# Two superblocks of a pair take turns over the shared blocks of x in the sort stage of a graph network kernel

## The reference

```python
# layer 0: a gated cell on summed messages, then a layer norm
src_h = h[src] @ W_msg.T + b_msg
msg = src_h + edge_embed[clip(edge_type)]
messages = segment_sum(msg, dst, N)
x = layernorm(x + gru_cell(messages, h))
# three further layers
ee = ea @ enc_w + enc_b
agg = segment_sum(concat(x[src], ee), dst, N)
h = relu(bn(agg @ w1 + b1)) @ w2 + b2
# with self loops; the result is layernorm(x + h)
```

## Time and profile before

| | us |
|---|---|
| median of 3 runs | 7135.25 |
| lowest, highest | 7131.29, 7141.64 |
| the profiled execution, its time | 7139.24 |
| its span | 7137.2 |
| first transpose of a unit starts | 273.7 |
| last scatter of the sort starts | 2344.6 |
| loads of the gathered records start | 2347.5 |

### The profile page before, as it was taken

How to read it: one execution, slowest core, us unless ns; L and a number is a source line. 1 busy time by engine, 2 the same in 40 slices (tenths; PEclk the granted TensorE clock), 3 DMA queues, 4 the chain that set the end, 5 groups by cost and what they waited for, 6 DMA issues and landing times.

```text
span 7137.2 us, 82504 instructions
## 1 busy us (share of the span) xinstructions
PE 5870.9 (82%) x29016; PEld 2854.1 (40%) x29152; DVE 3267.2 (46%) x8030; ACT 1370.1 (19%) x2496; POOL 5097.1 (71%) x4958
## 2 busy tenths in 40 slices
PE   2577777666677377767599999999999999999999
PEld 1233333333333143333344444444455444445444
DVE  5666666655565486676544444432222222222222
ACT  1233333333334121121111111110000000000000
POOL 3766666666667477777577777777777777777775
PEclk9998898888989587777699999999999999999999
DMA  6699999999999433333477778778878888778776
GB/s 222 161 238 245 236 240 239 244 240 243 250 242 254 121 99 97 99 99 98 137 240 240 236 229 247 236 242 258 243 233 254 245 243 269 240 241 241 242 240 191
DMA packets 1463508, 1536.87 MB, mean 215 GB/s; under 512 B 820755, under 2 KB 1202772, under 8 KB 1463100
## 3 DMA queue, kind: packets, MB, share of 16 engines
q1 hardware_dynamic: 1250604, 1182.45, 58.4%
q0 software_dynamic: 212496, 349.08, 19.2%
HBM read 1082.27 MB, written 281.76 MB: 191 GB/s over the span
## 4 chain that ended last, share of the span: by engine, by line
PE 53%; POOL 5%; DVE 3%; DMA 2%; issue 2%; ACT 1%; SPq 0%; ACTq 0%; DVEq 0%
PE ps L2502 34%; PE ps L2473 6%; POOL BIG L2556 5%; PE ps L2447 2%; PE ps L2446 2%; PE ps L2359 1%; PE ps L2431 1%; PE ps L2360 1%; PE ps L2453 1%; DMA XT<-rec_q 1%; PE ps L2454 1%; PE ps L2398 1%; DVE BIG L1883 1%; PE ps L2361 1%; DMA RECL<-rec_q 1%
## 5 line engine op out<-in xcount | busy, mean ns | idle before, releaser
L2574 POOL DMA_INDIRECT GL<-h_gathered,IDXA x2646 | 2700.7, 1021 | 919.5 <-issue 770.4
L2502 PE MATMUL ps<-MS,HP 128*128 128x512 bf16 (+1 forms) x11700 | 2712.0, 376 | 27.8 <-DMA MS<-counts 16.1
L2541 POOL DMA_INDIRECT rec_q<-BIG x1563 | 1562.7, 1000 | 777.5 <-issue 470.2
L2502 PEld LDWEIGHTS ps<-MS,HP 128*128 128x128 bf16 x11700 | 1132.7, 98 | 1251.9 <-issue 117.1
L2300 PE MATMUL ps<-MT,XPS 128*128 128x512 bf16 x3763 | 1082.7, 397 | 490.8 <-ACT MT L2102 281.0
L2556 POOL DMA_INDIRECT BIG<-x_parts,SRCq x739 | 828.9, 1122 | 290.1 <-issue 222.8
L2102 ACT CAST MT<-ps 128x512 bf16<-128x512 f32 x1274 | 735.9, 586 | 971.3 <-PE ps L2286 823.9
L1960 DVE TENSOR_REDUCE ROW<-ps 128x128 f32<-128x384 f32 x294 | 163.0, 554 | 1517.6 <-PE ps L2473 1517.6
L2300 PEld LDWEIGHTS ps<-MT,XPS 128*128 128x128 bf16 x3822 | 373.7, 101 | 983.9 <-ACT MT L2102 433.5
L2473 PE MATMUL ps<-GL,SL 128*128 128x384 bf16 (+1 forms) x2646 | 593.9, 333 | 26.0 <-DVE SL L1926 26.0
L2286 PE MATMUL ps<-BIG 128*128 128x512 bf16 x1197 | 470.1, 393 | 44.6 <-DVE BIG L1748 30.1
(11 more groups left out here) (198 smaller groups left out, 4982.6 us busy)
## 6 DMA issues: line engine op xcount, KB each, us to landing
MS<-counts SPq DMA_DIRECT2D x936, 512.0 KB, 4.7
counts<-BIG SPq DMA_DIRECT2D x312, 512.0 KB
XPS<-x_parts SPq DMA_DIRECT2D x312, 384.0 KB, 5.0
GL<-h_gathered,IDXA POOLq DMA_INDIRECT x2646
rec_q<-BIG POOLq DMA_INDIRECT x1563
rec_q<-BIG SPq DMA_DIRECT2D x44, 490.0 KB, 15.2
HTI<-h_cols SPq DMA_DIRECT2D x72, 256.0 KB, 5.9
BIG<-rec_q SPq DMA_DIRECT2D x13, 980.0 KB, 6.5
```

What stands on the lines that cost most here:

```text
L2502: got = t.matmul(bank[:, 0:w].rearrange("p (b c) -> p b c", c=P), HP[:, d, part, :], MS[:, i % MR, 0:x.nb, d % MB, :], start=d + part == 0 ...
L2541: g.indirect_dma_start(out=RAd, out_offset=bass.IndirectOffsetOnAxis(ap=POSI[:, c:c + 1], axis=0), in_=RECA[q % 3][:, c - a, :], in_offset ...
L2574: g.indirect_dma_start(out=GL[:, r % LR, i, 0:3 * P], out_offset=None, in_=HGd[lay], in_offset=bass.IndirectOffsetOnAxis(ap=IDXA[:, a + i: ...
```

## The change

Units are no longer numbered superblock by superblock. Superblocks 0 and 1, 2 and 3, up to 10 and 11 form pairs, and the units of a pair alternate: unit 0 of the first, unit 0 of the second, unit 1 of the first, and so on. Both use the same blocks of x, so one load serves both (`load`), and is issued at the first of the two. Superblock 12 has no partner. The sums of even superblocks stand in bank 6 and those of odd ones in bank 7, and ScalarE copies both at the next pair's first unit. The records of a pair come by halves, of 52 and of 46 cells of both superblocks (`HU` = 13 units), in buffers that are a little larger. Since a pair needs the records of its second superblock too, units begin in window 4 instead of window 3, and `PACE` is 47, so that windows hold 15 or 16 units and none is left after the last window.

```diff
-PACE = 44
+PACE = 47
+HU = 13
+class Unit:
+    def __init__(self, j, u, c0):
+        self.j, self.u, self.c0 = j, u, c0
+        self.n = min(4, NB - 4 * u)
+        self.pair = j // 2
+        self.load = SG * self.pair + u
+        self.half = 2 * self.pair + (u >= HU)
+        self.at = 4 * (u % HU)
+        self.first = j % 2 == 0
+def units():
+    got, c = [], 0
+    for j in range(0, JX, 2):
+        for u in range(SG):
+            for k in range(j, min(j + 2, JX)):
+                got.append(Unit(k, u, c))
+                c += got[-1].n
...
 def beside():
-            if w.q >= LAG:
+            if w.q > LAG:
                 work += PACE / w.groups
-            while m < SG * J and work >= (3 if m < SG * JX else 1) and m // SG <= w.q - LAG:
+            while m < len(UNITS) and work >= 3 and 2 * UNITS[m].pair + 1 <= w.q - LAG:
...
 def cells_scalar(s, m):
-                if u == 0 and i == 1 and 1 <= j <= JX:
-                    sums_scalar(s, j - 1)
+                if x.u == 0 and x.first and x.pair and i == 1:
+                    for j in range(x.j - 2, x.j):
+                        sums_scalar(s, j)
...
 def sums_tensor(t, c):
-                got = t.matmul(PS[7][:, :], XPS[:, m % 3, e % 4, part, :], ...
+                got = t.matmul(PS[6 + x.j % 2][:, :], XPS[:, x.load % 3, i, part, :], ...
...
 def cell_records_sync(y, k):
+            first = k // 2 * 2
+            if k % 2 == 0:
+                for q in range(max(0, first - 1), first + 3):
+                    y.wait_ge(scat[q % 3].sem, scattered(q))
...
 def cells_sync(y, m):
-            if u == 18 and j + 1 < J:
-                cell_records_sync(y, j + 1)
-            if m + 2 < SG * JX:
-                blocks_sync(y, m + 2)
+            if x.first:
+                if x.u == 4:
+                    cell_records_sync(y, 2 * x.pair + 1)
+                if x.u == 18 and 2 * x.pair + 2 < JX:
+                    cell_records_sync(y, 2 * x.pair + 2)
+                if x.load + 2 <= UNITS[-1].load:
+                    blocks_sync(y, x.load + 2)
```

More of the change, by code:

```diff
@@ L133, with last_unit, cells_to @@
 CARRY = carries()
+class Unit:
[7 more added lines that the diff above has]
+        self.first = j % 2 == 0
+        self.turn = None
+def units():
[5 more added lines that the diff above has]
+                c += got[-1].n
+    for s, x in enumerate(x for x in got if x.j < J):
+        x.turn = s
+    return got
+UNITS = units()
+TURNED = [x for x in UNITS if x.turn is not None]
+CELLS = [(m, i) for m, x in enumerate(UNITS) for i in range(x.n)]
+def last_unit(test):
+    return max(m for m, x in enumerate(UNITS) if test(x))
+def cells_to(m):
+    return UNITS[m].c0 + UNITS[m].n
 def beside():
@@ L141, in beside @@
             here = []
-            if w.q >= LAG:
+            if w.q > LAG:
                 work += PACE / w.groups
-            while m < SG * J and work >= (3 if m < SG * JX else 1) and m // SG <= w.q - LAG:
-                work -= 3 if m < SG * JX else 1
+            while m < len(UNITS) and work >= 3 and 2 * UNITS[m].pair + 1 <= w.q - LAG:
+                work -= 3
                 here.append(m)
@@ L148, in beside, with loaded, unit_turned @@
             at.append(here)
-    return at, list(range(m, SG * J))
+    return at, list(range(m, len(UNITS)))
 UNIT_AT, UNIT_REST = beside()
 XAT = {6 + 2 * i: i for i in range(SG)}
[L156 to L164, removed]
+def loaded(k):
+    return 16 * sum(min(2, JX - 2 * (e // 2)) for e in range(k % 2, k + 1, 2))
+def unit_turned(s):
+    return 16 * (s // 2 + 1)
 def scattered(q):
@@ L1471, in program @@
         RECA = [big(64 * RW).rearrange("p (c w) -> p c w", w=RW) for _ in range(3)]
-        recs0 = big(2 * NB * RW)
-        RECS = [recs0[:, NB * RW * i:NB * RW * (i + 1)].rearrange("p (c w) -> p c w", w=RW) for i in range(2)]
-        DSF = [big(NB) for _ in range(2)]
+        recs0 = big(2 * 2 * 4 * HU * RW)
+        RECS = [recs0[:, 8 * HU * RW * i:8 * HU * RW * (i + 1)].rearrange("p (j c w) -> p j c w", j=2, w=RW) for i in range(2)]
+        DSF = [big(8 * HU).rearrange("p (j c) -> p j c", j=2) for _ in range(2)]
         OHS = [big(GT * 64).bitcast(BF16).rearrange("p (c b) -> p c b", b=P) for _ in range(3)]
@@ L1730, in cells_vector @@
         def cells_vector(v, m):
[L1731 to L1736, removed]
+            x = UNITS[m]
+            k, par = x.half, x.j % 2
+            if x.at == 0 and x.first:
+                v.wait_ge(recs_in[k % 2].sem, loaded(k))
+                if k >= 2:
+                    v.wait_ge(ohd.sem, cells_to(last_unit(lambda y: y.half == k - 2)))
+                w = 4 * HU if k % 2 == 0 else NB - 4 * HU
+                for j in range(2 * x.pair, min(2 * x.pair + 2, JX)):
+                    v.tensor_scalar(DSF[k % 2][:, j % 2, 0:w], RECS[k % 2][:, j % 2, 0:w, 0].bitcast(I32), float(-512 * j), None,
+                                    ALU.add).then_inc(*dve.inc())
                 v.wait_ge(dve.sem, dve.total)
             if m >= 3:
[L1739 to L1745, removed]
+                v.wait_ge(mt.sem, cells_to(m - 3))
+            rel = RECS[k % 2][:, par, x.at:x.at + x.n, 1]
+            v.tensor_tensor(OHS[m % 3][:, 0:x.n, :], rel.unsqueeze(2).broadcast_to([P, x.n, P]),
+                            IOTA[:, :].unsqueeze(1).broadcast_to([P, x.n, P]), ALU.is_equal).then_inc(*ohs.inc())
+            for i in range(x.n):
+                c = x.c0 + i
                 if c >= 8:
                     v.wait_ge(mt.sem, c - 7)
-                v.tensor_scalar(OHD[c % 8], I512[:], DSF[j % 2][:, 4 * u + i:4 * u + i + 1], None,
+                v.tensor_scalar(OHD[c % 8], I512[:], DSF[k % 2][:, par, x.at + i:x.at + i + 1], None,
                                 ALU.is_equal).then_inc(*ohd.inc())
@@ L2093, in cells_scalar @@
         def cells_scalar(s, m):
-            j, u, c0, n = unit(m)
+            x = UNITS[m]
             if m >= 3:
[L2096 to L2100, removed]
+                y = UNITS[m - 3]
+                if y.turn is not None:
+                    s.wait_ge(turn_out[y.turn % 2].sem, unit_turned(y.turn))
+                s.wait_ge(xd.sem, cells_to(m - 3))
+            for i in range(x.n):
+                c = x.c0 + i
                 s.wait_ge(mt.sem, c + 1)
                 s.copy(MT[:, m % 3, 512 * i:512 * (i + 1)], PS[2 + c % 4][:, :]).then_inc(*mt_out.inc())
-                if u == 0 and i == 1 and 1 <= j <= JX:
-                    sums_scalar(s, j - 1)
+                if x.u == 0 and x.first and x.pair and i == 1:
+                    for j in range(x.j - 2, x.j):
+                        sums_scalar(s, j)
         def sums_scalar(s, j):
-            s.wait_ge(xd.sem, NB * (j + 1))
+            s.wait_ge(xd.sem, cells_to(last_unit(lambda y: y.j == j)))
             if j >= 2:
                 s.wait_ge(ad_out[j % 2].sem, 16 * (j // 2))
-            s.copy(XT[:, j % 2, :], PS[7][:, :]).then_inc(*acc_out.inc())
+            s.copy(XT[:, j % 2, :], PS[6 + j % 2][:, :]).then_inc(*acc_out.inc())
         def x_high(s, i):
@@ L2144, in sort_scalar @@
                 cells_scalar(s, m)
-            for j in range(J - 1, JX):
+            for j in range((JX - 1) // 2 * 2, JX):
                 sums_scalar(s, j)
@@ L2277, in cells_tensor @@
         def cells_tensor(t, m):
-            j, u, c0, n = unit(m)
+            x = UNITS[m]
             t.wait_ge(ohs.sem, m + 1)
-            for i in range(n):
-                c = c0 + i
+            for i in range(x.n):
+                c = x.c0 + i
                 t.wait_ge(ohd.sem, c + 1)
@@ L2290, in sums_tensor @@
         def sums_tensor(t, c):
-            j, e = c // NB, c % NB
-            m = SG * j + e // 4
+            m, i = CELLS[c]
+            x = UNITS[m]
             t.wait_ge(mt_out.sem, c + 1)
[L2295 to L2298, removed]
+            if i == 0:
+                t.wait_ge(xps_in[x.load % 3].sem, 16 * (x.load // 3 + 1))
+            if 4 * x.u + i == 0 and x.j >= 2:
+                t.wait_ge(acc_out.sem, x.j - 1)
             for part in range(3):
-                got = t.matmul(PS[7][:, :], XPS[:, m % 3, e % 4, part, :], MT[:, m % 3, 512 * (e % 4):512 * (e % 4 + 1)], start=e + part == 0,
-                               stop=e + part == NB + 1)
+                got = t.matmul(PS[6 + x.j % 2][:, :], XPS[:, x.load % 3, i, part, :], MT[:, m % 3, 512 * i:512 * (i + 1)],
+                               start=4 * x.u + i + part == 0, stop=4 * x.u + i + part == NB + 1)
             got.then_inc(*xd.inc())
@@ L2317, in sort_tensor @@
                 cells_tensor(t, m)
-            for c in range(NB * J - 2, NB * JX):
+            for c in range(len(CELLS) - 2, len(CELLS)):
                 sums_tensor(t, c)
@@ L2586, in attrs_sync, with cell_records_sync, blocks_sync @@
             y.dma_start(EAR[q % 2][:, 0:w.end - a, :], ea_v[:, a:w.end, :]).then_inc(*ea_in[q % 2].inc(16))
[L2588 to L2598, removed]
+        def cell_records_sync(y, k):
```

(39 more changed lines are left out.)

2 lines of the change are left out of this document (1 added, 1 removed).

## The result

The changed kernel takes 7095.43 us in the median of four runs (7094.65 to 7102.66), the kernel before 7136.97 in the same comparison. The ratio is 0.9946, with a 95% interval of 0.9931 to 0.9961. So it is 41 us faster, 0.5%. The forecast was 93 us faster: the gain is less than half of what was worked out. The time lies inside the whole range of 6975 to 7110, and outside the forecast's own 7008 to 7078.

What follows compares the result with a forecast made beforehand. The prediction took SyncE's full DMA queue to bound the sort: 185 us of saved loads less 93 for the later start moved window 23 by 93 us, 7139.24 to 7046, 7042 in median terms; range 6975 to 7110.

Steps and rivals of the forecast that it cites:

- The cost of the later start: Start of the sort: units wait for window 2's scatters too, 80.5 us later; rival 4 priced the whole pure loss at 92.
- The extra record issues: SyncE's queue: records in halves add two issues of some 0.4 us per pair, 3 us in all, inside the queue's drain.
- the holes: Each window's wait for the next attributes, issued late by SyncE: 11.9 us in windows 4 to 12, 9.9 in 13 to 23.
- rival 3: Sort windows: deeper prefetch removes PE's load waits, holes shrink, windows reach GpSimd's 83.8 us; 6934, partly near 6985; chance 14%.
- the first term: SyncE's queue in the sort: each x load left out saves 1.30 us, 175 loads in place of 325.
- The forecast for window 23: End of the sort: window 23 placed at 2124 instead of 2216.88, 93 us earlier, and the last scatter with it.
- The pitch of 5.64 us: SyncE's queue in steady state: a unit with its x load costs 5.64 us from one transpose's start to the next.
- Both readings behind 1.30: Load price: 5.64 less a 4.34 us no-load pitch near the end, and 393 KB at 304 GB/s, 1.29 us.
- My lower bound of 1.05: Least price of an x load, in us, from the best microsecond's 376 GB/s; the upper bound was 1.54.
- Rival 1: SyncE's own issuing bounds the sort, so a missing load saves only its 0.43 us issue and 0.1 behind; 7152; chance 10%.
- Rival 2: PE, ACT and VectorE set the pace in windows with 20 groups, costing 31 us more: 7073; chance 16%.
- Rival 4: x loads in the sort were hidden anyway, so the later start is pure loss: 92 us slower, 7227; chance 2%.

Runs made afterwards that it cites:

- e1: The kernel before with only the later start and PACE 47, still superblock by superblock with an x load each: 7230.2 us.
- e3: The changed kernel with each window's attributes loaded half a window earlier: 6971.4 us, ratio to before 0.9772.
- f5: e1 without any x load but the first three, rerun on another chip: pitch of transposes 4.81 us against 5.69 in e1.
- f6: e1 with only one of three parts of each x load, same rows and issues, rerun on another chip: two thirds of the bytes worth 0.53 us.
- e2: The changed kernel with only the first three x loads, all matmuls, transposes and stores kept: 6964.8 us, ratio 0.9759.
- e4: The kernel before with each window's attributes loaded half a window earlier: 7028.3 us, ratio 0.9848.
- f8: e1 with each store of counts made twice, the second to a spare tensor, rerun on another chip: the further store costs 1.10 us.
- f7: e1 with a plain copy of the same 512 KB in place of each DMA transpose, rerun on another chip: pitch 4.39 us.

## Why the prediction was right or wrong

**Right.** The bound, and where the end is set (window 23, then 99 scatters). The cost of the later start: 93 us measured in e1, 92 worked out. Window 4 at 426.8 for 424. Nothing after the sort moved. The extra record issues show in no wait. PE's waits for the copied sums are 18.7 us in six times (2.0 before), but e1, which copies one sum at a time, has 35.4, so the pairs did not make them. PE's waits for loads went from 159.8 to 20.2 us and the holes stayed, as the sum had it: the waits lay inside the queue's pace, and ScalarE's wait for transposes rose from 76.0 to 292.4 us. So rival 3 did not come; the holes went only in e3, by another cause.

**Wrong: the price of a load.** The step that failed is the first term, 1.30 us a load. The mechanism was right, a load adds its drain to a full queue, but the size was not. The runs give 0.95 (e1 against after), 0.88 (f5) and 0.80 (f6). The pitches of after against before give 0.46 a unit, thus 0.92 a load in pairs. With 142.5 loads by window 23, 1.30 against 0.95 is 50 us. The forecast for window 23 was missed by 49: 3 in window 4, 14 in windows 5 to 12 (738 us for 724), 33 in windows 13 to 23 (1009 for 976).

Two further errors cancelled, by luck. The pitch of 5.64 us was one reading, and the mean is 5.72: over the 298 units of windows 5 to 23 that is 24 us too little. What it left for the holes, 11.9 and 9.9 us a window, was 25 us too much beside the 9.4 of after.

Both readings behind 1.30 were of other places than the steady queue. The 4.34 us of the earlier trace rows are one pitch at the end of the stage. After shows the same there, while in mid-stage f5, with no loads at all, has 4.81 in the mean:

```profile
2245.84 3.32 SPq L2688 DMA_TRANSPOSE BIG<-MT  x1
2249.20 0.93 SPq L2695 DMA_DIRECT2D counts<-BIG  x1
2250.23 1.73 SPq L2688 DMA_TRANSPOSE BIG<-MT  x1
```

That is 4.39 us from start to start, as before. Between 430 and 2200 us the pitch into a transpose without a load ahead is 5.41 us and out of it 5.06. The prediction had looked for pitches alternating near 4.3 and 5.6. One unit's hold did fall as read, to 3.48 us, but the next one's rose from 4.39 to 4.63. A single neighbour says what its own hold is, not what the pair takes.

The 304 GB/s of the earlier trace rows are of a stretch with almost only plain loads, and I took the load's time there for its price here. Beside transposes 393 KB cost 0.85 us, which is 460 GB/s, more than the best microsecond of plain loads (376). The likely reading is that a part of a load's bytes flows in time that a transpose leaves unused; no run shows this directly. My lower bound of 1.05 was therefore no lower bound.

The estimate from the Trainium skill's 341 GB/s for a load of 1 MB (DMA: Bandwidth & Descriptors, section Bandwidth), 1.15 us, was nearer and still too high beside the 0.80 to 0.95 measured here.

**The holes** were sized well enough for the sum. With the mean pitches they are 94.7 - 14.67 x 5.72 = 10.8 and 93.0 - 14.73 x 5.72 = 8.7 us a window before, and 92.2 - 15.75 x 5.26 = 9.4 and 91.7 - 15.64 x 5.26 = 9.4 after.

**The rivals.** Rival 1 (slower) had its point of decision at 0.65 us a load; the measured prices are 0.15 to 0.3 above it, so the kernel came nearer to no gain than the sum said. Its mechanism, SyncE bound by its own issues, saves 0.53 a load, and e2 (0.82), f5 (0.88) and e1 against after (0.95) speak against it. Rival 2 doesn't show in after: windows with 20 groups (92.2) and with 16 (91.7) are alike. In f5 it begins to (86.1 and 83.9), where its 4.68 us a unit is only 0.2 below the pitch. Rival 4 was e1's time, 7227 worked out and 7230 measured, but of a kernel with all its loads.

## What to carry to other kernels

Price a transfer in a full queue by leaving it out or doubling it there, not by its time when it runs alone nor by one neighbour at the queue's end. Here the same bytes cost about 0.85 us in the queue, and 1.29 at the rate of loads by themselves. A change that pays a fixed cost first (93 us here) needs that price with its error, since the net gain is a difference of two large terms. And look for the load that stands last in an in-order queue behind work which doesn't need it: moving one attributes load per window half a window forward gave 109 us by itself (e4) and 124 on top of the reordering (e3), which gave 41.

## What the runs showed of the hardware

- Bytes of plain transfers added beside DMA transposes cost 0.82 us for 393 KB of stores (f8) and 0.80 to 0.88 for loads (f6, f5), with a DMA share near 1 in all. At the 304 GB/s of loads by themselves 393 KB take 1.29.
- A DMA transpose of 512 KB and the scatters beside it take 3.7 us of a full queue, a store of the same size 1.10.
- The same transpose holds SyncE 2.05 us on an empty queue, in the full one 3.48 without and 4.63 with a load ahead (after); a plain copy of the same bytes holds it 0.6 (f7).
- Copies in place of transposes brought the share to 0.84 at 288 GB/s (f7), from 1.03 at 243 (e1).
- A full DMA share does not say that bytes flow at the best rate: 213, 231, 243 and 269 GB/s stood beside shares of 0.97, 1.00, 1.03 and, with the stores doubled (f8, below), 1.03.

```profile
430.00:2000.00 1570.00, 974.34 (x4346) 437.04 (x4431) 787.00 (x2158) 489.44 (x855) 828.13 (x838) 0.86 1.03 269
```

- One chip ran the kernel before in 9302 us where three comparisons on others had 7134 to 7137, with idle spells of up to 25 us that no record explains.
